# Mask rows on every eighth partition, and three larger mask transfers issued by ScalarE in place of nine by SyncE

## The chip, the cores and the metric

The kernel runs on one core of a Trainium2 chip. The metric is the device time of one execution in microseconds (us). A core has TensorE (PE: matrix products into PSUM), VectorE (DVE), ScalarE (ACT), GpSimd (POOL) and SyncE (SP, which here only issues DMAs), all running their own instruction streams in order and meeting at semaphores, and 16 DMA engines that all queues share.

## The reference, cut to what matters

```python
def _dcnv4(x, dw_w, dw_b, om_w, om_b, vp_w, vp_b, op_w):     # x: 8 images of 16 x 16 x 64
    xdw = depthwise_3x3(x, dw_w) + dw_b
    om = (xdw @ om_w + om_b).reshape(n, h, w, G, KK * 3)      # G = 8 groups, KK = 9 taps
    offset = om[..., :2 * KK].reshape(n, h, w, G, KK, 2)
    mask = om[..., 2 * KK:]
    value = (x @ vp_w + vp_b).reshape(n, h, w, G, GC)
    ...                                                       # bilinear sample of value at the offsets
    out = einsum('nhwgkc,nhwgk->nhwgc', sampled, mask).reshape(n, h, w, c)
    return out @ op_w

x = x + _dcnv4(groupnorm(x), ...)
t = x as tokens
t = t + attention(layernorm(t))
t = t + mixture_of_experts(layernorm(t))
```

The change touches only the convolution with offsets (`_dcnv4`), and of it the way in which `mask`, one number for each pixel, group and tap, comes from the product `om` to the place where it is multiplied in.

## The kernel before, in words

`conv_stage` works through the eight images one after the other; `token_stage` (attention and experts) follows behind a barrier. While image i is sampled, the tables of image i+1 are made, so each engine runs the same pattern once per image:

- PE (`image`, L445): nine steps v. Each has `sample(v)` (L382, or L387 for the last tap), which multiplies the x-interpolation weights `b` with the values `vt` into the PSUM ring `ps_t`; `reduce(v-1)` (L402, L406), which sums DVE's products; and two slots of `JOBS` for image i+1: the two halves of the offset product `om` (`offsets`, L292), the values (L303, on every second image), the output product of image i-1 (L314), and nine replications (`replicate`, L323) that spread offset rows over the partitions.
- DVE (`weight`, L684 and L688): 18 products w per image of `ps_t` with the y-interpolation weights in `a_rep`; two per step v. On every second image nine taps of the depthwise convolution (L658, L661) lie between them.
- ACT: `copy_offsets` (L508) brings `om` from PSUM to `om_f` with the bias; `high_offsets` (L516) rounds it to `om_r`; `copy_d` (L548); then for each replication a copy with absolute value (L530, L533) and a `hat` (L542), which turns it into a weight in `a` (y) or `b` (x).
- POOL: `low_offsets` (L756), the remainder of the rounding; `tables` (L767); and `masked(k)` (L777), which multiplies the taps of pair k of `a` by `mask`. Five pairs k hold the nine taps.
- SP: `masks(n)` (L247), nine DMAs that spread eight rows (one for each group) of `om_f` to all 128 partitions of `mask`, 128 KB each in elements of 1 KB; then `fill(n)` (L259), 20 DMAs that spread the masked `a` to `a_rep`, 16 of 256 KB in elements of 2 KB and four of 128 KB.

So the chain of one image is: `om` product, `om_f`, mask DMA and (beside it) replication and hat, `masked`, fill DMA, `weight`. `a`, `mask` and `om_f` have one buffer each; `a_rep` and `b` have two. `copy_offsets(0, n)` waits until the masks of image n-1 have been read (`mask_in`) and applied (`a_done`). The order on each engine is written out by hand. `P` is 128 partitions, `PIX` 256 pixels, `QUADS` 3.

Of the kernel before, what the change touches and what calls it, by code (L numbers as in the profile page):

```python
# [31 lines left out]
P = 128  # L32
IMAGES, H, W, C = 8, 16, 16, 64
PIX = H * W
TT = IMAGES * PIX // P
TPI = PIX // P
GROUPS = 8
GC = C // GROUPS
TAPS = 9
# [4 lines left out]
QUADS = 3  # L44
SLABS = IMAGES // 2
SELS = 6
ROWS = 120
BANK = 512
PAIRS = (TAPS + 1) // 2
BATCHES = TAPS  # L50
# [39 lines left out]
def conv_stage(nc, d, t_tok, pack, pack_in):  # L90

    with ExitStack() as ctx:
# [81 lines left out]
        a_hat = sem("a_hat")  # L175
        a_done = sem("a_done")
        b_done = sem("b_done")
        mask_in = [sem(f"mask_in{k}") for k in range(PAIRS)]
        a_filled = [[sem(f"a_filled{k}_{h}") for h in range(2)] for k in range(PAIRS)]
        sampled = sem("sampled")  # L180
        weighted = sem("weighted")
# [28 lines left out]

            return len(REPS) * n + r - len(BY_DVE)

        def mask_rows(k):

            return [(tap, tap // 3, (48, 56, 112)[tap % 3]) for tap in range(2 * k, min(2 * k + 2, TAPS))]

        def masks_in(k, images):

            return 16 * len(mask_rows(k)) * images

        def pair_taps(k):

            return slice(2 * k, min(2 * k + 2, TAPS))
# [7 lines left out]
        @block.sync  # L231
        def _(sp):
            sp.dma_start(x_turned[:, :, :, :].rearrange("p s y x -> p (s y x)"), d["x_turned"]).then_inc(x_in, 16)
            sp.dma_start(keep[:, :], d["keep"]).then_inc(keep_in, 16)
            sp.dma_start(start[:, :], d["start"]).then_inc(start_in, 16)
            sp.dma_start(t_tok[:, :, :], xview).then_inc(tokens_in, 16)
            sp.dma_start(pack[:, :], d["attention"]).then_inc(pack_in, 16)

            def masks(n):

                halves = [count(sp, 2 * n + half + 1) for half in range(2)]
                for k in range(PAIRS):
                    if k in (0, 3):
                        sp.wait_ge(om_copied, halves[k // 3])
                    for tap, q, row in mask_rows(k):
                        src = om_f[row:row + GROUPS, q, :]
                        sp.dma_start(mask[:, tap, :], src.unsqueeze(1).broadcast_to([GROUPS, P // GROUPS, PIX]))\  # L247
                          .then_inc(mask_in[k], 16)

            def fill(n, par):  # L250

                used = count(sp, WPI * (n - 1))
                if positive(used):
                    sp.wait_ge(weighted, used)
                for k in range(PAIRS):
                    sp.wait_ge(a_done, PAIRS * n + k + 1)
                    for m in range(DUOS):
                        src = a[32 * m:32 * m + 32, pair_taps(k), :]
                        sp.dma_start(a_rep[par][:, m, pair_taps(k), :],  # L259
                                     src.unsqueeze(1).broadcast_to([32, 4, src.shape[1], PIX]))\  # L260
                          .then_inc(a_filled[k][m // 2], 16)

            masks(0)
            fill(0, 0)
            masks(1)
            fill(1, 1)
            with sp.Fori(1, IMAGES // 2) as it:
                for par in range(2):
                    masks(2 * it + par)
                    fill(2 * it + par, par)  # L270

        @block.tensor
# [207 lines left out]
        def _(act):  # L480
# [16 lines left out]
            def copy_offsets(half, n):  # L497
                act.wait_ge(om_ps, 2 * n + half + 1)
                if positive(2 * n + half - 1):
                    act.wait_ge(om_low, 2 * n + half - 1)  # L500
                if positive(n):
                    for k in (range(3) if half == 0 else range(3, PAIRS)):
                        act.wait_ge(mask_in[k], masks_in(k, n))
                    if half == 0:
                        act.wait_ge(a_done, PAIRS * n)
                bank = ps_m[:, :] if positive(n) else ps_t[0][:, half, :]
                for q in range(2 - half):
                    op = act.activation(om_f[0:ROWS, 2 * half + q, :], bank[0:ROWS, q * PIX:(q + 1) * PIX],  # L508
                                        ACT.Identity, bias=om_bias[0:ROWS, 2 * half + q:2 * half + q + 1])
                op.then_inc(om_copied, 1)  # L510

            def high_offsets(half, n):
                act.wait_ge(om_copied, 2 * n + half + 1)
# [71 lines left out]
            def image(i, par, slab, made):  # L585
                n, npar = i + 1, 1 - par
                if made:
                    copy_offsets(0, n)
                    high_offsets(0, n)
                last = None if isinstance(i, int) and i == 0 else i - 1  # L590
                if LAG == 1 and last is not None:
                    copy_d(last)
                if made:
                    copy_offsets(1, n)
                    high_offsets(1, n)
                if LAG == 2 and last is not None:
                    copy_d(last)
                if made:
                    reps(n, npar, slab)
# [9 lines left out]
            high_offsets(0, 0)  # L609
            copy_offsets(1, 0)  # L610
            high_offsets(1, 0)
            first_reps()
            image(0, 0, 1, True)
            image(1, 1, None, True)
# [127 lines left out]
        @block.gpsimd  # L742
        def _(pool):
            pool.memset(minus_half[:, :], -0.5).then_inc(zeroed, 1)
            pool.memset(xpad[:, :, :, :], 0.0).then_inc(zeroed, 1)
            pool.wait_ge(zeroed, 2)
            pool.wait_ge(gn_steps, 5)
            pool.tensor_tensor(grstd[:, :], gvar_eps[:, :], minus_half[:, :], ALU.pow).then_inc(gn_pow, 1)

            def low_offsets(half, n):  # L750

                if half == 0 and positive(n):
                    pool.wait_ge(a_done, PAIRS * n)
                pool.wait_ge(om_high, 2 * n + half + 1)
                q = slice(2 * half, 2 + half)
                pool.tensor_tensor(om_r[64:ROWS, q, :], om_f[64:ROWS, q, :], om_r[64:ROWS, q, :].bitcast(F32),  # L756
                                   ALU.subtract).then_inc(om_low, 1)

            def tables(n, par, slab):

                pool.wait_ge(keep_in, 16)
                pool.wait_ge(om_low, 2 * n + 2)
                pool.wait_ge(v_done, slab + 1)
                if positive(WPI * (n - 1)):
                    pool.wait_ge(sampled, WPI * (n - 1))
                for j in range(DUO):
                    op = pool.tensor_tensor(vt[par][:, :, j, :, :].rearrange("p h y c -> p y h c"),  # L767
                                            v_sb[:, :, par, j, :].rearrange("p y (h c) -> p y h c", h=2),
                                            spread(spread(spread(rows[:, j], 1, H), 2, 2), 3, 4), ALU.mult)
                op.then_inc(vt_ready, 1)  # L770

            def masked(k, n, par):

                pool.wait_ge(a_hat, PAIRS * n + k + 1)
                pool.wait_ge(mask_in[k], masks_in(k, n + 1))
                v = a[:, pair_taps(k), :]
                pool.tensor_tensor(v, v, mask[:, pair_taps(k), :], ALU.mult).then_inc(a_done, 1)  # L777

            def image(n, par, slab):
                low_offsets(0, n)  # L780
                low_offsets(1, n)
                tables(n, par, slab)
                for k in range(PAIRS):
                    masked(k, n, par)

            image(0, 0, 0)
            image(1, 1, 0)
            image(2, 0, 1)
            with pool.Fori(1, IMAGES // 2 - 1) as it:
                image(2 * it + 1, 1, it)  # L790
                image(2 * it + 2, 0, it + 1)
            image(IMAGES - 1, 1, SLABS - 1)
# [736 lines left out]
def shape_arrays(np):  # L1529
# [10 lines left out]
    at = np.arange(P)  # L1540
    for which in range(SELS):
        for part in (0, 64):
            sel[part + 8 * which + at // 16, which, at] = 1.0
        if which < 3:
            sel[ROWS, which], sel[ROWS + 1, which] = -(at % 16), 1.0
        else:
# [4 lines left out]
    grid[ROWS + 2] = np.arange(W)[None, :]  # L1551
    kernel_at = np.zeros((P, QUADS), np.float32)
    for q in range(QUADS):
        for row, tap, kind in places(q):
            kernel_at[row:row + 8, q] = (tap % 3 - 1, tap // 3 - 1, 0)[kind]

    select = np.zeros((P, EXPERTS // 2, 2, C), np.float32)
    for e in range(EXPERTS):
# [8 lines left out]
def places(q):  # L1567

    y, x, m = 1, 0, 2
    spots = [(part + 8 * (3 * at + r), 3 * q + r, kind) for part in (0, 64) for at, kind in enumerate((y, x))  # L1570
             for r in range(3)]
    return spots + [(row, 3 * q + r, m) for r, row in enumerate((48, 56, 112))]

def laid_out(inputs, np):
# [6 lines left out]
    om_w = np.zeros((C, QUADS, P), om.dtype)  # L1582
    om_b = np.zeros((P, QUADS), bias.dtype)
    for q in range(QUADS):
        for row, tap, kind in places(q):
            j = 2 * TAPS + tap if kind == 2 else 2 * tap + kind
            om_w[:, q, row:row + 8] = om[:, :, j]
            om_b[row:row + 8, q] = bias[:, j]
    op = f["L0_conv_op_w"].reshape(DUOS, DUO, 2, 4, C).transpose(0, 2, 1, 3, 4)
    op_w = np.zeros((DUOS, 32, C), op.dtype)  # L1590
    op_w[:, 0:16] = op.reshape(DUOS, 16, C)
# [50 lines left out]
```

## Time and profile before

| | us |
|---|---|
| median of three runs | 498.77 (496.94 to 500.3) |
| the profiled execution, its own time | 497.56 |
| its span in the trace | 495.8 |
| PE, DVE, ACT, POOL busy | 409.9, 331.0, 238.3, 136.7 |

Of the span, the eight images of the convolution take what lies between the first DVE product at 35.3 us and the last at 292 us. The profiled execution is 1.2 us under the median; sums below are made against 497.56 and then moved to the median. A PE that is busy for 83% of the span is not a PE at its peak: its matmuls are pipelined, and the profile also shows stretches in which it was granted half its clock.

### The profile page before, as it was taken

To read this page: it belongs to the slowest core of one execution; us is meant where nothing else is said; L and a number is where in the kernel's file an instruction comes from. 1 tells how busy PE (TensorE), PEld (TensorE's weight loads), DVE (VectorE), ACT (ScalarE), POOL (GpSimd) and SP (SyncE) were. 2 spreads that over 40 slices of the span, in tenths; PEclk is the share of its full clock that TensorE was granted. 3 is DMA by queue.
4 is the path that set the end of the run, shared out by engine and by line. 5 is a ranking of instruction groups with operands and counts; after the bars stand their busy time and mean duration, and the time that the engine had idled before them with its cause. 6 is when DMAs were issued, how large, how long until landed. Compare 5 with 4: busy or idle time off the path is not lost. (4 is left out here: it accounts for less than half of the span.)

```text
span 495.8 us, 9559 instructions
## 1 busy us (share of the span) xinstructions
PE 409.9 (83%) x3188; PEld 223.2 (45%) x3188; DVE 331.0 (67%) x725; ACT 238.3 (48%) x528; POOL 136.7 (28%) x172
## 2 busy tenths in 40 slices
PE   0749969879799699895993854798999999999995
PEld 0612333322343233432330223586767767777673
DVE  3408937669488378693873864576876868667653
ACT  3542523435425235354260004457677676767752
POOL 1251240421502404215022004513323323233322
PEclk9958979989889789898896995569999999999998
DMA  6169488586684875966857705000000000000000
GB/s 207 39 156 236 122 210 204 125 226 166 164 238 111 208 201 117 231 157 163 220 123 201 210 14 240 1 1 1 1 1 13 2 0 3 12 0 3 12 0 13
DMA packets 38200, 53.94 MB, mean 109 GB/s; under 512 B 7440, under 2 KB 20880, under 8 KB 37904
## 3 DMA queue, kind: packets, MB, share of 16 engines
q1 hardware_dynamic: 38160, 53.44, 41.9%
q8 instruction: 22, 0.36, 0.3%
q14 instruction: 18, 0.15, 0.1%
HBM read 5.71 MB, written 0.52 MB: 13 GB/s over the span
## 5 line engine op out<-in xcount | busy, mean ns | idle before, releaser
L684 DVE TENSOR_TENSOR prod<-ps_t,a_rep 128x1024 f32<-128x1024 f32 x128 | 152.3, 1219 | 74.7 <-DMA a_rep<-a 55.1
L382 PE MATMUL ps_t<-b,vt 32*128 32x512 f32 x512 | 81.7, 710 | 13.8 <-DVE prod L684 13.6
L777 POOL TENSOR_TENSOR a<-a,mask 128x512 f32<-128x512 f32 (+1 forms) x40 | 46.7, 1170 | 155.2 <-DMA mask<-om_f 137.1
L402 PE MATMUL ps_d<-prod,keep 128*32 128x512 f32 x512 | 74.3, 655 | 2.7 <-DVE prod L684 2.5
L1231 POOL TENSOR_TENSOR total<-total,share 128x256 f32<-128x256 f32 x56 | 40.9, 731 | 87.3 <-DVE share L1125 86.9
L1109 DVE TENSOR_TENSOR hidden<-ps_h,gated 128x256 f32<-128x256 f32 x128 | 51.4, 415 | 3.7 <-ACT gated L1324 2.4
L1324 ACT ACTIVATE gated<-ps_h 128x256 f32<-128x256 f32 x128 | 47.9, 388 | 7.4 <-PE ps_h L1444 1.1
L530 ACT ACTIVATE a<-ps_m 128x512 f32<-128x512 f32 x28 | 16.7, 597 | 67.8 <-PE ps_m L323 67.8
L1444 PE MATMUL ps_h<-xf,w_h 128*128 128x256 f32 x128 | 43.7, 342 | 2.0 <-ACT gated L1324 2.0
L1125 DVE TENSOR_TENSOR share<-ps_yf,factor 128x256 f32<-128x256 f32 x56 | 23.7, 424 | 30.8 <-issue 12.8
L1318 ACT ACTIVATE factor<-ps_yf 128x256 f32<-128x256 f32 x64 | 24.7, 386 | 37.5 <-PE ps_yf L1479 37.5
L1479 PE MATMUL ps_yf<-hidden,w 128*64 128x256 f32 x256 | 41.9, 405 | 0.0
L323 PEld LDWEIGHTS ps_m<-om_r,sel 128*128 128x128 f32 x128 | 19.5, 192 | 48.3 <-issue 32.2
L382 PEld LDWEIGHTS ps_t<-b,vt 32*128 32x128 f32 x512 | 21.9, 198 | 42.0 <-DVE prod L684 29.8
L292 PE MATMUL ps_m<-conv,start 64*128 64x256 f32 x42 | 15.4, 479 | 26.5 <-ACT om_f L508 23.9
L1444 PE MATMUL ps_h<-xf,w_l 128*128 128x256 f32 x128 | 36.7, 287 | 0.0
L1444 PEld LDWEIGHTS ps_h<-xf,w_h 128*128 128x128 f32 x128 | 24.7, 193 | 26.6 <-issue 21.2
L1453 PE MATMUL ps_h<-xf,w_h 128*128 128x256 f32 x128 | 36.5, 286 | 0.0
L1453 PE MATMUL ps_h<-xf,w_l 128*128 128x256 f32 x128 | 36.4, 285 | 0.0
L323 PE MATMUL ps_m<-om_r,sel 128*128 128x256 f32 x128 | 32.6, 337 | 0.0
L530 ACT ACTIVATE b<-ps_m 128x512 f32<-128x512 f32 x28 | 16.7, 598 | 28.9 <-PE ps_m L323 28.9
L1475 PE MATMUL ps_yf<-dispatch,select 128*128 128x256 f32 x64 | 23.8, 371 | 5.8 <-DVE t_tok L1131 3.3
(149 smaller groups left out, 644.0 us busy)
## 6 DMA issues: line engine op xcount, KB each, us to landing
a_rep<-a SPq DMA_DIRECT2D x128, 256.0 KB, 4.6
mask<-om_f SPq DMA_DIRECT2D x72, 128.0 KB
a_rep<-a SPq DMA_DIRECT2D x32, 128.0 KB, 3.2
w_f<-in_w SPq DMA_DIRECT2D x2, 1024.0 KB, 5.7
start<-in_start SPq DMA_DIRECT2D x1, 960.0 KB, 7.3
x_turned<-in_x_turned SPq DMA_DIRECT2D x1, 512.0 KB, 3.4
t_tok<-in_x SPq DMA_DIRECT2D x1, 512.0 KB, 8.7
w<-in_w SPq DMA_DIRECT2D x1, 512.0 KB, 7.6
```

What stands on the lines that cost most here:

```text
L323: mm = pe.matmul(bank[:, s * PIX:(s + 1) * PIX], sel[:, tap % 3 + 3 * axis, :], om_r[:, tap // 3, :], start=True, stop=True)
L382: mm = pe.matmul(out, vt[par][r, v % 2, :, :, :].rearrange("p j y c -> p (j y c)"), b[par][r, pair_taps(v // 2), :].rearrange("p t x -> p ...
L402: mm = pe.matmul(ps_d[r, :], fold[:, v % 2, :], p, start=v == 0, stop=False, skip_group_check=True)
L530: act.activation(dst[:, pair_taps(k), :].rearrange("p t x -> p (t x)"), ps_m[:, :], ACT.Abs)\
L684: dve.tensor_tensor(p[:, :, :], t[:, :, :], a_rep[par][:, ms, pair_taps(v // 2), :].rearrange("p m t x -> p m (t x)"), ALU.mult).then_inc( ...
L777: pool.tensor_tensor(v, v, mask[:, pair_taps(k), :], ALU.mult).then_inc(a_done, 1)
L1109: dve.tensor_tensor(hidden[u % 4][:, :], ps_h2[u % 2][:, 0:PIX], gated[u % 4][:, :], ALU.mult)\
L1231: pool.tensor_tensor(sums[:, :], sums[:, :], share[p % 2][:, :], ALU.add).then_inc(added, 1)
L1324: act.activation(gated[u % 4][:, :], ps_h1[u % 2][:, 0:PIX], ACT.Silu).then_inc(silu_done, 1)
L1444: mm = pe.matmul(ps_h1[u % 2][:, 0:PIX], w[:, e, :], tokens, start=first, stop=not first)
L1453: mm = pe.matmul(ps_h2[u % 2][:, 0:PIX], w[:, e, :], tokens, start=first, stop=not first)
L1479: mm = pe.matmul(ps_y[64 * k:64 * k + 64, :], w3[:, u % EXPERTS, :], hidden[u % 4][:, :], start=True, stop=True)
```

## The change

The mask rows of `om_f` move. Before, tap t had its eight group rows on eight neighbouring partitions (48, 56 or 112 on), in column block t // 3. Now the rows of one third of the taps (three taps, one column block each) lie on partitions 0, 8, ..., 56, on 1, 9, ..., 57 or on 64, 71, ..., 113, and the offset rows take the partitions in between (`PLACE_ROWS`). Thus three taps are contiguous on a partition, and one DMA carries 3 KB elements for three taps: three DMAs an image of 384 KB each. They are issued by ACT, behind the rounding of the second half of the offsets, and wait for both halves. SP keeps the fills alone. Matmuls, activations and products keep their number and shapes.

```diff
+MASK_ROWS = [slice(0, 64, 8), slice(1, 64, 8), slice(64, 114, 7)]
+PLACE_ROWS = {0: [r for r in range(64) if r % 8 > 1], 64: [r for r in range(64, 120) if r % 7 != 1 or r > 113]}
...
-        mask_in = [sem(f"mask_in{k}") for k in range(PAIRS)]
+        mask_in = [sem(f"mask_in{j}") for j in range(QUADS)]
...
-            def masks(n):
-
-                halves = [count(sp, 2 * n + half + 1) for half in range(2)]
-                for k in range(PAIRS):
-                    if k in (0, 3):
-                        sp.wait_ge(om_copied, halves[k // 3])
-                    for tap, q, row in mask_rows(k):
-                        src = om_f[row:row + GROUPS, q, :]
-                        sp.dma_start(mask[:, tap, :], src.unsqueeze(1).broadcast_to([GROUPS, P // GROUPS, PIX]))\
-                          .then_inc(mask_in[k], 16)
...
             with sp.Fori(1, IMAGES // 2) as it:
                 for par in range(2):
-                    masks(2 * it + par)
                     fill(2 * it + par, par)
...
-                if positive(n):
-                    for k in (range(3) if half == 0 else range(3, PAIRS)):
-                        act.wait_ge(mask_in[k], masks_in(k, n))
-                    if half == 0:
-                        act.wait_ge(a_done, PAIRS * n)
+                if positive(n) and half == 0:
+                    for j in range(QUADS):
+                        act.wait_ge(mask_in[j], 16 * n)
+                    act.wait_ge(a_done, PAIRS * n)
...
+            def masks(n):
+
+                act.wait_ge(om_copied, 2 * n + 2)
+                for j in range(QUADS):
+                    src = om_f[MASK_ROWS[j], :, :].rearrange("g q x -> g (q x)")
+                    act.dma_start(mask[:, QUADS * j:QUADS * (j + 1), :].rearrange("p q x -> p (q x)"),
+                                 src.unsqueeze(1).broadcast_to([GROUPS, P // GROUPS, QUADS * PIX])).then_inc(mask_in[j], 16)
...
                 if made:
                     copy_offsets(1, n)
                     high_offsets(1, n)
+                    masks(n)
...
-                pool.wait_ge(mask_in[k], masks_in(k, n + 1))
+                for j in range(2 * k // QUADS, min(2 * k + 1, TAPS - 1) // QUADS + 1):
+                    pool.wait_ge(mask_in[j], 16 * (n + 1))
```

On SP, in the loop over images (`mask<-om_f` is a mask DMA, `a_rep<-a` a fill), one image began like this before:

```order
L247 DMA mask<-om_f 128x1x256 [waits om_copied]
L247 DMA mask<-om_f 128x1x256 x5
L244 REGISTER_ALU
L247 DMA mask<-om_f 128x1x256 [waits om_copied]
L247 DMA mask<-om_f 128x1x256 x2
L254 ISA
L256 ISA [waits weighted]
L259 DMA a_rep<-a 128x1x512 [waits a_done]
L259 DMA a_rep<-a 128x1x512 x3
```

Of these nine rows four stay, at the same place of SP's loop in the changed kernel:

```order
L248 UNCONDITIONAL_BRANCH
L248 ISA
L239 ISA [waits weighted]
L242 DMA a_rep<-a 128x1x512 [waits a_done]
L242 DMA a_rep<-a 128x1x512 x3
```

The nine mask issues are gone from SP; the fills keep their number, order and waits.

On ACT, at the seam between two images (`om_f` and `om_r` are the offsets and their rounding, `d_sb` the sums of the image before, `a<-ps_m` the first replication), the loop had before:

```order
L548 ACTIVATE d_sb<-ps_d 128x512 [waits out_ps]
L498 REGISTER_ALU
L503 REGISTER_ALU [waits mask_in3,om_low,om_ps]
L508 ACTIVATE om_f<-ps_m,om_bias 120x256 [waits mask_in4]
L516 ACTIVATE om_r<-om_f 120x256 [waits rep_ps,om_copied]
L522 REGISTER_ALU
L530 ACTIVATE a<-ps_m 128x512 [waits a_filled0_1,a_filled0_0,rep_ps]
```

And in the changed kernel:

```order
L535 ACTIVATE d_sb<-ps_d 128x512 [waits out_ps]
L478 REGISTER_ALU
L487 ACTIVATE om_f<-ps_m,om_bias 120x256 [waits om_low,om_ps]
L503 ACTIVATE om_r<-om_f 120x256 [waits rep_ps,om_copied]
L496 DMA mask<-om_f 128x1x768 [waits om_copied]
L496 DMA mask<-om_f 128x1x768 x2
L509 REGISTER_ALU
L512 REGISTER_ALU [waits rep_ps]
L517 ACTIVATE a<-ps_m 128x512 [waits a_filled0_1,a_filled0_0]
```

Three DMA issues stand now between the rounding of the second half and the copy of the first replication, and the waits for the masks of the image before have moved ahead of the first half.

## Rows read from the trace of the kernel before

**Rows 1.** Waits, whole span: us in total, times, longest

```profile
POOL a L777 <- DMA mask<-om_f: 137.1, 37, 19.1
DVE prod L684 <- DMA a_rep<-a: 55.1, 15, 11.1
```

**Rows 2.** Timeline of DVE: start, us, instruction, [idle before <-releaser]

```profile
35.31 1.22 DVE L684 TENSOR_TENSOR prod<-ps_t,a_rep 128x1024 f32<-128x1024 f32 x1 [11.15 <-DMA a_rep<-a]
...
142.52 2.36 DVE L684 TENSOR_TENSOR prod<-ps_t,a_rep 128x1024 f32<-128x1024 f32 x2 [0.72 <-PE ps_t L382]
...
167.02 1.23 DVE L684 TENSOR_TENSOR prod<-ps_t,a_rep 128x1024 f32<-128x1024 f32 x1 [6.47 <-DMA a_rep<-a]
...
176.38 1.23 DVE L684 TENSOR_TENSOR prod<-ps_t,a_rep 128x1024 f32<-128x1024 f32 x1 [1.67 <-PE ps_t L382]
...
267.05 1.23 DVE L684 TENSOR_TENSOR prod<-ps_t,a_rep 128x1024 f32<-128x1024 f32 x1 [8.22 <-DMA a_rep<-a]
269.06 1.22 DVE L684 TENSOR_TENSOR prod<-ps_t,a_rep 128x1024 f32<-128x1024 f32 x1 [0.79 <-DMA a_rep<-a]
```

**Rows 3.** Timeline of SP's DMA issues, merged by line

```profile
161.06 21.09 SPq L259 DMA_DIRECT2D a_rep<-a  x20
182.28 11.53 SPq L247 DMA_DIRECT2D mask<-om_f  x9
194.01 21.83 SPq L259 DMA_DIRECT2D a_rep<-a  x20
```

**Rows 4.** Tile mask: its issues' length in ns, min/median/max

```profile
L247 SPq DMA_DIRECT2D mask<-om_f x72: 619/1250/1847, 18.0 to 259.9; - x72
```

**Rows 5.** Windows: busy by engine, then PEclk, DMA share, GB/s

```profile
161.10:182.10 21.00, 16.50 (x92) 6.41 (x92) 10.82 (x13) 5.71 (x11) 5.68 (x7) 0.76 0.85 219
182.30:193.80 11.50, 10.75 (x82) 3.70 (x80) 11.43 (x13) 6.25 (x13) 2.55 (x2) 1.00 0.47 103
```

**Rows 6.** Timeline of PE round two seams between images

```profile
141.25 1.14 PE L382 MATMUL ps_t<-b,vt 32*128 32x512 f32 x8
...
159.90 1.14 PE L382 MATMUL ps_t<-b,vt 32*128 32x512 f32 x8
160.97 1.13 PE L292 MATMUL ps_m<-conv,start 64*128 64x256 f32 x4
162.03 1.09 PE L406 MATMUL ps_d<-prod,keep 128*32 128x256 f32 x16
166.45 0.70 PE L292 MATMUL ps_m<-conv,start 64*128 64x256 f32 x2 [3.33 <-ACT om_f L508]
168.30 2.09 PE L382 MATMUL ps_t<-b,vt 32*128 32x512 f32 x8 [1.16 <-DVE prod L684]
...
195.38 1.14 PE L382 MATMUL ps_t<-b,vt 32*128 32x512 f32 x8
...
202.54 1.94 PE L303 MATMUL ps_m<-keep,xv 128*32 128x32 f32 x128
...
205.48 1.10 PE L314 MATMUL ps_m<-keep,d_sb 128*128 128x64 f32 x8
```

**Rows 7.** Timeline of ACT: the prologue, then the seam at 165 us

```profile
20.93 0.60 ACT L557 ACTIVATE a<-ps_t 128x512 f32<-128x512 f32 x1 [1.49 <-PE ps_t L323]
...
34.61 0.84 ACT L508 ACTIVATE om_f<-ps_m,om_bias 120x256 f32<-120x256 f32 x2 [6.15 <-POOL a L777]
...
168.02 0.42 ACT L516 ACTIVATE om_r<-om_f 120x256 fp32r<-120x256 f32 x1
177.02 0.60 ACT L530 ACTIVATE a<-ps_m 128x512 f32<-128x512 f32 x1 [8.58 <-PE ps_m L323]
177.65 0.63 ACT L542 ACTIVATE a<-a 128x512 f32<-128x512 f32 x1
```

**Rows 8.** Timeline of POOL, first pair of the image of rows 7

```profile
188.33 1.28 POOL L777 TENSOR_TENSOR a<-a,mask 128x512 f32<-128x512 f32 x1 [18.03 <-DMA mask<-om_f]
```

**Rows 9.** Page, part 6: issues, KB each, median us to landing

```profile
a_rep<-a SPq DMA_DIRECT2D x128, 256.0 KB, 4.6
```

More of the change, by code:

```diff
@@ L211, in outs @@
             return len(REPS) * n + r - len(BY_DVE)
[L213 to L219, printed above, removed]
         def pair_taps(k):
@@ L261, in fill @@
                           .then_inc(a_filled[k][m // 2], 16)
-            masks(0)
             fill(0, 0)
-            masks(1)
             fill(1, 1)
@@ L611, in _ @@
             high_offsets(1, 0)
+            masks(0)
             first_reps()
@@ L1542, in shape_arrays @@
         for part in (0, 64):
-            sel[part + 8 * which + at // 16, which, at] = 1.0
+            sel[np.array(PLACE_ROWS[part])[8 * which + at // 16], which, at] = 1.0
         if which < 3:
@@ L1553, in shape_arrays @@
     for q in range(QUADS):
-        for row, tap, kind in places(q):
-            kernel_at[row:row + 8, q] = (tap % 3 - 1, tap // 3 - 1, 0)[kind]
+        for spots, tap, kind in places(q):
+            kernel_at[spots, q] = (tap % 3 - 1, tap // 3 - 1, 0)[kind]
     select = np.zeros((P, EXPERTS // 2, 2, C), np.float32)
@@ L1569, in places @@
     y, x, m = 1, 0, 2
-    spots = [(part + 8 * (3 * at + r), 3 * q + r, kind) for part in (0, 64) for at, kind in enumerate((y, x))
-             for r in range(3)]
-    return spots + [(row, 3 * q + r, m) for r, row in enumerate((48, 56, 112))]
+    spots = [(PLACE_ROWS[part][8 * (3 * at + r):8 * (3 * at + r + 1)], 3 * q + r, kind) for part in (0, 64)
+             for at, kind in enumerate((y, x)) for r in range(3)]
+    return spots + [(MASK_ROWS[j], 3 * j + q, m) for j in range(QUADS)]
 def laid_out(inputs, np):
@@ L1584, in laid_out @@
     for q in range(QUADS):
-        for row, tap, kind in places(q):
+        for spots, tap, kind in places(q):
             j = 2 * TAPS + tap if kind == 2 else 2 * tap + kind
-            om_w[:, q, row:row + 8] = om[:, :, j]
-            om_b[row:row + 8, q] = bias[:, j]
+            om_w[:, q, spots] = om[:, :, j]
+            om_b[spots, q] = bias[:, j]
     op = f["L0_conv_op_w"].reshape(DUOS, DUO, 2, 4, C).transpose(0, 2, 1, 3, 4)
```

## The prediction, on record before the changed kernel ran

> **What bounds the kernel now.** I read the waits first. The longest of the whole span is POOL's, for the mask DMA, and DVE's longest is for the fill [rows 1]: both ends of one DMA queue. So I followed that queue. SP's timeline has no hole [rows 3]: 20 fill issues from 161.06 us for 21.09 us, nine mask issues from 182.28 for 11.53, the next fill at 194.01. One turn is 32.95 us. DVE's first product of an image starts at 35.31 us for the first image and at 267.05 for the last [rows 2]: 231.74 / 7 = 33.11 us for an image. The queue's turn is the image's period; everything else waits for it.
>
> It is not the issuing itself that takes the time. A mask issue takes 0.62 us at least and 1.25 in the median [rows 4], so SP is held back while earlier transfers drain. And in the mask stretch the 16 DMA engines are busy for 0.47 of the time and move 103 GB/s, against 0.85 and 219 GB/s in the fill stretch [rows 5]. Transfers in one queue go in order, so for a third of the period half of the DMA capacity lies idle while the fills stand behind the masks.
>
> What the stall does further on: POOL stood ready for 18.03 us until the first mask came [rows 8], while the hat that it multiplies was done at 177.65 + 0.63 = 178.3 us [rows 7]. DVE then waited 6.47 us for the fill, and PE restarted slowly: a step of eight matmuls took 2.09 us at 168.30, 1.14 before and later [rows 2, 6, 7]. In that fill stretch the granted clock averages 0.76 against 1.00 in the mask stretch [rows 5], that is, part of it ran at 1.2 GHz and not 2.4, after PE had stood still.
>
> **The period when DMA is not late.** I put it together from full-clock pieces of PE [rows 6], sample(0) of an image to sample(0) of the next. From sample(0) to sample(2): 1.07 us (159.90 to 160.97), the first offset product 1.06, the last reduce 1.09, then the second offset product, which must wait for ACT's 0.84 us copy [rows 7]: I put its end 0.2 us after the reduce. Then 0.70, sample(1) 1.07, reduce(0) another 1.09, the output product 1.10 less the 0.07 by which steps overlap (159.90 + 1.14 against 160.97): 7.3 us in all. On odd images the values add 1.94. From sample(2) to the next sample(0) nothing waits for DMA today: 141.25 to 159.90 is 18.65 us on an odd image. On an even one, with DVE's nine convolution taps, the product w4 starts at 176.38 [rows 2]; w4 follows sample(2) by 1.27 us (142.52 against 141.25), so it is 175.11 to 195.38, 20.27 us. Odd: 7.3 + 1.94 + 18.65 = 27.9. Even: 7.3 + 20.27 = 27.6. Mean 27.75 us, against 33.11: **5.36 us an image, seven times: 37.5 us.**
>
> **Is the DMA then fast enough?** The sum of engine time in rows 5: the fill is 0.85 x 21.0 = 17.9 us on all 16. If the 0.47 of the mask stretch means about half of the engines fully busy, the masks are 0.94 x 11.5 = 10.8 us on that half. If the two overlap, the busier half has 28.7 us of work an image, even if 3 KB elements gain nothing. That is 1 us over 27.75, and there is a lead to eat first: pair 0 was ready for masking at 178.3 and its fill went out at 194.01 [rows 3, 7]. With masks there early the fill goes out by about 180, some 14 us sooner, while DVE's turn comes only 5.4 us sooner. Some 8 us of lead against 1 us an image lasts through eight images. I take nothing for it; the bound above is 7 us.
>
> **What moves to ACT.** Three issues after the rounding of the second half, ahead of the first replication's copy. No row shows a DMA issued by ACT. The nearest rows are SP's: three at 0.62 are 1.9 us, at 1.25 3.75 us, at 1.85 5.5 us [rows 4]. What hides them: ACT sat idle for 8.58 us at just this place [rows 7], but most of that was PE standing still. Without the stall it is shorter. The rounding ends 1.3 us after the second offset product (168.44 against 167.15 [rows 6, 7]). The first replication's copy starts 0.64 us after w4 (177.02 against 176.38 [rows 2, 7]), so 1.9 us after sample(2) starts. Between lie sample(1), reduce(0) and the output product: ACT has 1.07 + 1.09 + 1.03 + 1.9 - 1.3 = 3.8 us on even images and 5.7 on odd ones. At the median nothing is lost, at the longest 1.7 us on each of four even images; queued behind a late ACT stand the first replication's copy, through it PE's next use of `ps_m`, and the hat for POOL. I take 1 us for all images, with bounds of 0 and 7.
>
> **Ends of the stage.** First image: ACT's rounding ends at 20.93 - 1.49 = 19.44 us, where SP began the masks at 18.0 [rows 4, 7], and ACT has those 1.49 us idle for 1.9 us or more of issues. The fills no longer stand behind nine masks, which draws DVE's first product forward. But the offsets of image 1 wait for POOL's last masking (34.61 us [rows 7]), and that for about the same mask bytes. I take 0, with bounds of 3 us either way. Last image: the 0.79 us wait for a fill at 269.06 goes [rows 2]: 0.8 us. The waits for three `mask_in` that moved ahead of the first half are met long before, and matmuls, activations and products are the same: nothing. The token stage is untouched.
>
> **Sum.** 37.5 + 0.8 - 1 = 37.3 us. From the profiled execution's 497.56 that is 460.3; the median is 1.2 above it, so **461 us**.
>
> **Rivals.** A: the DMA engines stay the bound. The fill's share of 0.85 speaks for it [rows 5]: there is little room beside the fills, and if the masks take that room one for one the turn stays fill plus mask. The mask part would be at most today's 11.5 us and at least its bytes at the fill's rate, 1.18 MB / 219 GB/s = 5.4 us (then there is no bound). The middle, 9.5 us, gives 21.4 + 9.5 = 31 us an image, 15 us gained, **484 us**; with 11.5 us the change does nothing, 498. Against it: the idle half in the mask stretch.
>
> The Trainium skill has the rule for this rival (DMA: Bandwidth & Descriptors, section Issuing engines are not separate DMA queues): transfers from several engines run on the same 16 DMA engines and interleave, so a second issuer saves only sequencer time. By that rule the result is A. The trace does not bear out its premise in the mask stretch, where the share is 0.47. My estimate from that page is 3.6 + 3.6 + 2.1 = 9.3 us for the three DMAs alone, where nine took 11.5; no row here shows the new layout.
>
> B: ACT becomes the late one, and the time ends **slower**. Place: the third issue at each seam. Mechanism: ACT's queue takes an issue only when the one before has landed. A 256 KB fill lands 4.6 us after its issue [rows 9]; at no less for 384 KB ACT is held 0.6 + 2 x 4.6 = 9.8 us, 6.0 more than the even images have and 4.1 more than the odd ones: 5.05 us an image, nearly the whole gain. Each such stall also leaves PE at half clock for a while, as today; I put that at 2 us a seam, two steps at 2.09 for 1.14, so 498.8 - 37.3 + 7 x 7.05 = **511 us**. It turns slower where ACT is held for more than 4.75 + 5.36 - 2 = 8 us on average. Against it: SP today takes three issues in less than that with 1.25 us in the median.
>
> C: the masks go out as said, but ACT is held at its upper bound and the 28.7 us bind as well: 461 + 6 (beyond the 1 us taken) + 7 = **474 us**.
>
> **How the numbers follow.** Forecast (450 to 470): 0.60. A: 0.22, a quarter of it within 1% of 498.8. B: 0.08, a quarter of it within 1%. C: 0.07. Faster than 450, if the steps at the seam overlap better than my chain of PE: 0.03. 1%, or 5 us, is about what a measurement of this kernel can tell from no change. So faster 0.60 + 0.16 + 0.07 + 0.03 = 0.86, same 0.08, slower 0.06. For the range, the lower bound is 461 less 3 us at the first image, 1 us of ACT and 1 us a seam: 450. Up it takes in C and the better half of A, to 486: above lie 0.11 of A and 0.08 of B.
>
> **What would show it.** SP's timeline should have fills only, with pauses between images in which it waits for POOL. POOL's wait for the mask DMA should fall from 137 us to under 30, and DVE's waits for `a_rep` to the first image alone. PE's full-clock stretches should join, and DVE's first products should be 27 to 29 us apart. The first copy of a replication on ACT should follow the mask issues with little or no PE wait behind it. SP without a pause and a period of 30 us or more would mean A; a PE wait for ACT's copy at `ps_m` at each seam would mean B or C. I am wrong if the periods at the seams contain a wait that DMA now hides, such as POOL's remainder of the rounding ahead of the first replication.

## The result, and the profile after

The changed kernel took 480.0 us in the median of four runs (479.04 to 481.95), the kernel before 499.53 us on the same chip: a ratio of 0.9615, with a 95% interval of 0.9556 to 0.9674. The time lies inside the whole range of 450 to 486 us, but outside the forecast's own 450 to 470, and the gain is 19.5 us where 37.8 were forecast, about half. Of the cases, rival A (the DMA engines stay the bound, 484 us) is the nearest. The profiled execution took 481.95 us, the longest of the four; its span is 480.0, 15.8 under the span before, and it is these 15.8 us that are accounted for below.

The waits of the changed kernel (us in total, times, longest) answer to [rows 1]:

```profile
POOL a L767 <- DMA mask<-om_f: 74.6, 17, 6.5
DVE prod L673 <- PE ps_t L362: 43.0, 44, 9.3
ACT a L517 <- DMA a_rep<-a: 37.8, 7, 7.2
ACT a L517 <- issue: 33.5, 6, 6.6
...
PEld ps_m L303 <- ACT a L517: 27.7, 12, 5.8
```

POOL's wait for the masks fell from 137.1 us to 74.6, not to under 30, and DVE's 55.1 us of waiting for `a_rep` are no longer among the long ones. Two new waits stand before ACT's first copy of a replication. One is for its own DMA issues (`issue`). The other is for fills: `a` has one buffer, and the copy into it must wait until the fill of the image before has read it. PE then waits for ACT at `ps_m`, and DVE for PE at `ps_t`.

SP's timeline, from the first fill to the last, and from the first fill of the last image, answers to [rows 3]:

```profile
26.40 236.95 SPq L242 DMA_DIRECT2D a_rep<-a  x160
...
242.18 21.17 SPq L242 DMA_DIRECT2D a_rep<-a  x20
```

And SP's waits for the masked `a` (total, times, longest):

```profile
SPq L242 <- POOL a L767: 24.1, 8, 17.6
```

The longest of these waits, 17.6 us, stands before the first fill; the other seven are 6.5 us together, so from then on SP issues 160 fills almost without a pause. From the first fill of the first image to that of the last is (242.18 - 26.40) / 7 = **30.8 us an image**; only the last image, with no masks beside it, still takes 21.17 us, as the fills did alone [rows 3]. The masks are gone from SP's queue, and the turn of the fills has become longer by 30.8 - 21.2 = 9.6 us an image, against 11.53 us when the masks stood in front of them. The tile `mask` (length of its issues in ns, min/median/max), now on ACT, answers to [rows 4]:

```profile
L496 ACTq DMA_DIRECT2D mask<-om_f x24: 602/1329/4411, 19.2 to 225.7; - x24
```

ACT's timeline at a seam answers to [rows 7]:

```profile
131.99 6.72 ACTq L496 DMA_DIRECT2D mask<-om_f  x3
...
138.96 0.60 ACT L517 ACTIVATE a<-ps_m 128x512 f32<-128x512 f32 x1 [6.56 <-issue]
...
150.76 0.60 ACT L517 ACTIVATE a<-ps_m 128x512 f32<-128x512 f32 x1 [5.05 <-DMA a_rep<-a]
```

The queue does hold ACT: one issue takes up to 4.41 us, three take 6.72. Now DVE's first products of the first and of the last image, which answer to [rows 2]:

```profile
33.69 1.23 DVE L673 TENSOR_TENSOR prod<-ps_t,a_rep 128x1024 f32<-128x1024 f32 x1 [9.34 <-PE ps_t L362]
...
69.03 2.36 DVE L673 TENSOR_TENSOR prod<-ps_t,a_rep 128x1024 f32<-128x1024 f32 x2
...
252.87 4.81 DVE L673 TENSOR_TENSOR prod<-ps_t,a_rep 128x1024 f32<-128x1024 f32 x4 [0.56 <-PE ps_t L362]
```

The period is (252.87 - 33.69) / 7 = 31.3 us, before 33.11 and forecast 27.75. The first of the seven took 35.3 us (to 69.03, the first product of the second image), the other six 30.6 in the mean, the turn of the fills. That is 12.6 us gained in seven periods. The first product comes 1.6 us earlier (35.31 to 33.69), and from the last image's first product to the end of the span it is 480.0 - 252.87 = 227.1 us against 495.8 - 267.05 = 228.75, another 1.6. Together 15.8 us, the difference of the two spans. Last, three windows answer to [rows 5]: one over more than five images, one in which masks are in flight beside the fills (their packets run from 134.6 to 148.7 us), and one in which the fills are alone:

```profile
75.00:250.00 175.00, 154.69 (x1358) 59.45 (x1352) 133.46 (x131) 75.52 (x147) 49.87 (x52) 0.96 0.82 192
...
135.20:149.20 14.00, 13.20 (x95) 4.18 (x94) 11.33 (x11) 4.62 (x8) 3.98 (x4) 1.00 0.79 177
119.00:132.00 13.00, 10.76 (x86) 4.65 (x86) 10.46 (x11) 8.82 (x19) 3.00 (x3) 1.00 0.87 211
```

And the DMA queues of the page (packets, MB, time as a share of 16 engines' span):

```profile
q1 hardware_dynamic: 28368, 44.00, 37.6%
q10 hardware_dynamic: 3264, 9.44, 8.1%
```

Beside the masks the two kinds of transfer together move 177 GB/s at a share of 0.79, less than the fills do alone (211 GB/s, 0.87), and the masks' packets are in flight for 14.6 us of each image (images 1 to 7, by the times of the 3 KB packets). Queue q10, ACT's, holds the masks only: 0.081 x 16 x 480.0 / 8 = 77.8 us of engine time an image.

### The profile page after: what moved, and what is told of

The parts are those of the page before. It is cut to its first block and busy times, and to the rows that moved or that the text cites. A ratio compares the mean times of both kernels' runs of the same rounds, so it can differ in the third digit from the quotient of the medians.

```text
span 480.0 us, 9496 instructions
## 1 busy us (share of the span) xinstructions
PE 401.7 (84%) x3188; PEld 221.1 (46%) x3188; DVE 332.5 (69%) x725; ACT 237.4 (49%) x528; POOL 136.7 (28%) x172
## 5 line engine op out<-in xcount | busy, mean ns | idle before, releaser
L362 PE MATMUL ps_t<-b,vt 32*128 32x512 f32 x512 | 77.8, 678 | 2.9 <-DVE prod L673 2.7
L382 PE MATMUL ps_d<-prod,keep 128*32 128x512 f32 x512 | 71.9, 634 | 6.6 <-DVE prod L673 6.4
L767 POOL TENSOR_TENSOR a<-a,mask 128x512 f32<-128x512 f32 (+1 forms) x40 | 46.9, 1179 | 104.3 <-DMA mask<-om_f 74.6
L517 ACT ACTIVATE a<-ps_m 128x512 f32<-128x512 f32 x28 | 16.7, 597 | 85.3 <-DMA a_rep<-a 37.8
L303 PEld LDWEIGHTS ps_m<-om_r,sel 128*128 128x128 f32 x128 | 20.3, 200 | 68.3 <-ACT a L517 27.7
L303 PE MATMUL ps_m<-om_r,sel 128*128 128x256 f32 x128 | 33.8, 347 | 17.5 <-ACT a L517 17.5
L1308 ACT ACTIVATE factor<-ps_yf 128x256 f32<-128x256 f32 x64 | 24.6, 385 | 37.9 <-PE ps_yf L1469 37.9
L362 PEld LDWEIGHTS ps_t<-b,vt 32*128 32x128 f32 x512 | 21.2, 192 | 29.7 <-DVE prod L673 17.7
L745 POOL TENSOR_TENSOR om_r<-om_f,om_r 56x512 fp32r<-56x512 f32 (+1 forms) x16 | 15.9, 1002 | 57.3 <-ACT om_r L503 57.2
```

What stands on the lines that cost most here:

```text
L303: mm = pe.matmul(bank[:, s * PIX:(s + 1) * PIX], sel[:, tap % 3 + 3 * axis, :], om_r[:, tap // 3, :], start=True, stop=True)
L362: mm = pe.matmul(out, vt[par][r, v % 2, :, :, :].rearrange("p j y c -> p (j y c)"), b[par][r, pair_taps(v // 2), :].rearrange("p t x -> p ...
L382: mm = pe.matmul(ps_d[r, :], fold[:, v % 2, :], p, start=v == 0, stop=False, skip_group_check=True)
```

## The experiments

Theory A: the DMA engines bound the period, and the masks take room from the fills one for one; then the masks' cost is set by what they cost the engines, above all by where their source rows lie. Theory B: ACT, held by its issues, starts the replications late. Theory C: the one buffer of `a` makes ACT wait for the fills, and a second one gives the time back. Theory P, which the later expectations test, is a form of A: the DMA engines that carry a mask meet at the ports through which they read its rows. Each of the ten runs was timed in three rounds beside the kernel before on the same chip.

**The floor: masks for the first image alone.** The masks of images 1 to 7 are not sent; those of image 0 stay in `mask`.

```diff
-                    masks(n)
...
-                    pool.wait_ge(mask_in[j], 16 * (n + 1))
+                    pool.wait_ge(mask_in[j], 16)
```

> Leaves out the mask DMAs of images 1 to 7 (they are multiplied with the masks of image 0). Theory A, the DMA engines are the bound (fills alone take some 21 us an image in the kernel before, 29.6 with masks beside them in the changed one): the fills fit again, SP pauses between images, and DVE's first products come 27 to 28.5 us apart instead of 31.3, some 455 us. Theory B, ACT's hold of 6.7 us on its three issues is the bound: the same 455, for the hold goes too; only SP's pauses and the waits for a_rep differ. Theory C, the single buffer a is the bound whatever the masks do (copy of the first factor waits for the fill of the image before): little change, 475 to 480, ACT still waits for a_rep. If it stays over 460 my chain of PE steps at the seam (27.75 us an image) was wrong too.

456.16 us, ratio 0.9132 (0.9094 to 0.917). SP's timeline, the fills of the last image:

```profile
211.60 20.89 SPq L242 DMA_DIRECT2D a_rep<-a  x20
```

DVE's timeline, the first products of the first and of the last image:

```profile
33.72 1.23 DVE L672 TENSOR_TENSOR prod<-ps_t,a_rep 128x1024 f32<-128x1024 f32 x1 [9.33 <-PE ps_t L362]
...
227.07 4.81 DVE L672 TENSOR_TENSOR prod<-ps_t,a_rep 128x1024 f32<-128x1024 f32 x4 [0.61 <-PE ps_t L362]
```

SP's waits for the masked `a`:

```profile
SPq L242 <- POOL a L766: 57.1, 11, 19.2
```

And a window (busy by engine, PEclk, DMA share, GB/s):

```profile
75.00:220.00 145.00, 138.64 (x1275) 53.07 (x1271) 124.67 (x122) 71.96 (x139) 46.29 (x48) 1.00 0.71 174
```

The period is (227.07 - 33.72) / 7 = 27.6 us: the chain of PE that the prediction put together (27.75) is the bound once DMA is out of the way, at a granted clock of 1.00. The last image's fill starts 15.5 us ahead of its first product, against 10.7 us in the changed kernel (252.87 - 242.18) and 7.3 in its first image (33.69 - 26.40). So here the fills run ahead, and SP pauses: 37.9 us in ten waits behind the first, against 6.5 in the changed kernel. Theory C, which expected 475 to 480 us, is already against this; A and B are not parted, for ACT's issues went together with the transfers.

**Two buffers of `a`.** The changed kernel with `a` doubled by the image's parity, and semaphores of the fills for each.

```diff
-        a = sb("a", [P, TAPS, PIX])
+        a = [sb(f"a{i}", [P, TAPS, PIX]) for i in range(2)]
...
```

> Two buffers for a, used by turns, so that a copy of a replication waits for the fill two images back. Theory A: the queue of fills still needs 29.6 us an image with masks beside it, SP has no pause, but the lag can now build up over several images: 29.6 to 30 us an image at most, 466 to 470 us, ACT's waits for a_rep gone and DVE's waits for a_rep back in their place. Theory B: ACT's hold stays, 476 to 480. Theory C: the full forecast, 455 to 462.

480.2 us, ratio 0.9626 (0.9583 to 0.9668): no change against 480.0. ACT's waits for `a_rep` are gone from the list, and SP's issues take as long as before:

```profile
26.35 236.36 SPq L242 DMA_DIRECT2D a_rep<-a  x160
```

Theory C falls: the wait for the buffer was only the form in which the late fills showed. Theory A's own number for this run, 466 to 470 us, was missed; the time stands in theory B's range of 476 to 480, and it takes the issues spread, below, to part the two.

**The mask rows back on neighbouring partitions.** Still three DMAs of 3 KB elements, issued by ACT.

```diff
+MASK_ROWS = [slice(48, 56), slice(56, 64), slice(112, 120)]
+PLACE_ROWS = {0: list(range(48)), 64: list(range(64, 112))}
```

> Undoes the spreading alone: the mask rows back on eight neighbouring partitions (48, 56 and 112 on), still three DMAs of 3 KB elements issued by ACT. If the place of the rows matters to the transfer, the masks take longer in flight than 14.4 us and hold the fills more: with the 11.3 us of the kernel before in place of the 8.9 that they now cost the fills, 2.4 us an image, 495 us. If it does not matter: 480 within 3.

549.15 us, ratio 1.0976 (1.0917 to 1.1034): 69 us slower than the changed kernel, with the same bytes, DMAs and issuer, and far beyond both expected numbers (480 and 495). SP's timeline, all fills and those of the last image:

```profile
29.91 302.47 SPq L242 DMA_DIRECT2D a_rep<-a  x160
...
310.57 21.81 SPq L242 DMA_DIRECT2D a_rep<-a  x20
```

The masks' queue on the page:

```profile
q10 hardware_dynamic: 3264, 9.44, 12.8%
```

The turn of the fills is (310.57 - 29.91) / 7 = 40.1 us, and 0.128 x 16 x 547.8 / 8 = 140 us of engine time an image for the masks, against 77.8.

**The new rows and sizes, issued by SP as before.** `masks(n)` stands ahead of `fill(n)` in SP's loop again.

```diff
+                    sp.dma_start(mask[:, QUADS * j:QUADS * (j + 1), :].rearrange("p q x -> p (q x)"),
...
+                    masks(2 * it + par)
                     fill(2 * it + par, par)
...
-                    act.dma_start(mask[:, QUADS * j:QUADS * (j + 1), :].rearrange("p q x -> p (q x)"),
...
```

> Undoes the move to ACT alone: three DMAs of 3 KB elements from spread rows, issued by SP at the old place, all before the fills of the image. If the size and the place of the rows shorten the masks by themselves, the mask stretch of SP falls from 11.3 to some 9 us and the period from 33.1 to 31: about 484. If only the second queue helps: 498 within 4.

477.59 us, ratio 0.9549 (0.95 to 0.9599), no slower than the changed kernel, and better than the 484 that was expected. SP's timeline:

```profile
141.10 4.08 SPq L238 DMA_DIRECT2D mask<-om_f  x3
148.05 22.73 SPq L250 DMA_DIRECT2D a_rep<-a  x20
170.92 3.93 SPq L238 DMA_DIRECT2D mask<-om_f  x3
```

The window of the mask stretch between two fills:

```profile
141.10:148.00 6.90, 6.90 (x52) 1.76 (x48) 5.92 (x6) 4.10 (x9) 1.26 (x1) 1.00 0.53 120
```

The turn shown is 170.92 - 141.10 = 29.8 us, and the mean of seven turns 30.4, although masks and fills stand in one queue. So the part of the change that moved the issues from SP to ACT brought nothing; the whole gain is in the three DMAs and their rows.

**ACT's issues spread.** The second and third issue stand behind the first and the second replication.

```diff
+                    if r in (1, 2):
+                        masks(n, [r])
...
-                    masks(n)
+                    masks(n, [0])
```

> The three issues on ACT no longer stand together: the first behind the rounding, the second behind the first replication's copy, the third behind the third replication's. Theory B, ACT's hold of 6.7 us at the seam costs PE time: the hold shrinks to 2 or 3 us in pieces and the time falls to about 470. Theory A, the DMA engines are the bound and the hold is covered by them: 480 within 3, SP without a pause as before.

481.06 us, ratio 0.9664 (0.9589 to 0.974). The tile's issues:

```profile
L496 ACTq DMA_DIRECT2D mask<-om_f x24: 601/612/2471, 19.5 to 229.3; - x24
```

The median issue is 0.61 us in place of 1.33, the longest 2.47 in place of 4.41, and the time is the same. Theory B falls: holding ACT cost nothing while the DMA was late anyway. (The spread also sends two of the masks later; the next run, with the three issues together again, says the same without that.)

**Rows on every fourth partition, issued by ACT.**

```diff
+MASK_ROWS = [slice(0, 32, 4), slice(1, 32, 4), slice(64, 96, 4)]
+PLACE_ROWS = {0: [r for r in range(64) if r >= 32 or r % 4 > 1], 64: [r for r in range(64, 120) if r >= 96 or r % 4]}
```

> As the changed kernel, with the mask rows on every fourth partition (0 to 28, 1 to 29, 64 to 92). Theory P, the masks cost the fills time because several of the eight engines that carry a mask read over the same SBUF ports: with a port for each row the masks' stay in flight falls from 14.4 us to under 11, the fills take 27 to 28 us an image with masks beside them, 460 to 468 us. Rival, they cost it because eight engines carry mask and fill in turn, whatever the ports: 480 within 3.

455.96 us, ratio 0.9138 (0.9065 to 0.9211): 24 us faster than the changed kernel, on the floor of 456.16 and below the 460 to 468 that theory P expected. SP's timeline, all fills and those of the last image:

```profile
25.90 215.23 SPq L242 DMA_DIRECT2D a_rep<-a  x160
...
218.15 22.99 SPq L242 DMA_DIRECT2D a_rep<-a  x20
```

The same window as for the floor:

```profile
75.00:220.00 145.00, 137.99 (x1267) 53.04 (x1263) 122.60 (x122) 71.02 (x138) 45.99 (x47) 1.00 0.87 214
```

The masks' queue on the page:

```profile
q10 hardware_dynamic: 3264, 9.44, 6.7%
```

The turn of the fills is (218.15 - 25.90) / 7 = 27.5 us, just under PE's 27.75, and the rate beside the masks is 214 GB/s where the changed kernel moved 192. The masks cost 0.067 x 16 x 455.8 / 8 = 61 us of engine time an image.

**The same rows, issued by SP.** The rows of this and the issuer of the fourth experiment.

> The same rows with the three DMAs issued by SP at the old place. Theory P: the stretch from the first mask issue to the first fill falls from 7.2 us to some 5 and the turn of SP from 30.3 to 28, 462 to 467 us, where 477.6 was measured with rows on every eighth partition. Rival, masks that run alone are not limited by the ports but by landing and by POOL: 477 within 3.

454.32 us, ratio 0.9132 (0.9061 to 0.9203), below the expected 462 to 467: the same as with ACT, although here the masks stand ahead of the fills. SP's timeline:

```profile
129.72 2.58 SPq L238 DMA_DIRECT2D mask<-om_f  x3
136.12 20.47 SPq L250 DMA_DIRECT2D a_rep<-a  x20
156.73 2.65 SPq L238 DMA_DIRECT2D mask<-om_f  x3
```

The window of the mask stretch:

```profile
129.70:136.00 6.30, 6.30 (x50) 2.14 (x46) 5.54 (x6) 3.33 (x6) 1.20 (x1) 1.00 0.54 151
```

The turn shown is 27.0 us, the mean of seven 27.5; the mask stretch moves 151 GB/s at nearly the share of 0.53 that moved 120.

**Nine DMAs from the rows of the changed kernel, issued by SP.** Against the kernel before the rows differ, and with them the order in which they are read (three DMAs in a row from one set); all nine also wait for both halves of the offsets.

```diff
+                for tap in range(TAPS):
+                    src = om_f[MASK_ROWS[tap // 3], tap % 3, :]
+                    sp.dma_start(mask[:, tap, :], src.unsqueeze(1).broadcast_to([GROUPS, P // GROUPS, PIX]))\
+                      .then_inc(mask_in[tap // 3], 16)
...
```

> Nine DMAs of 1 KB elements as in the kernel before, from the spread rows (every eighth partition), issued by SP. It parts the place of the rows from the size of the elements. If the place alone brings the gain: 478 to 482. If the size alone: 495 to 499. If each brings part: between, some 488.

481.29 us, ratio 0.9656 (0.9583 to 0.9729): nearly the whole gain of the change, with DMAs no larger than before. So the gain comes with the rows, not with the size.

**Three DMAs from neighbouring partitions, issued by SP.** The 24 rows are those of the kernel before, and so is the issuer; what differs is the size of the DMAs, with it which taps lie on one row and are read together, and that all wait for both halves.

> The mask rows on eight neighbouring partitions as in the kernel before, SP issues as before, only three DMAs of 3 KB elements in place of nine of 1 KB. If the size of the elements brings nothing by itself: 495 to 501. If larger elements shorten the masks: 485 to 492. If one DMA from few partitions at a time is slower than several from different ones in flight together: over 505.

561.21 us, ratio 1.1254 (1.1165 to 1.1344): with these rows the larger DMAs are a loss of 63 us against the 498.47 measured beside them. Against the new rows in the same three DMAs from SP (477.59), where the rows alone differ, they are a loss of 84 us. SP's timeline:

```profile
141.50 6.56 SPq L238 DMA_DIRECT2D mask<-om_f  x3
152.24 28.88 SPq L250 DMA_DIRECT2D a_rep<-a  x20
181.66 6.50 SPq L238 DMA_DIRECT2D mask<-om_f  x3
```

The window of the mask stretch, which moves 78 GB/s at a share of 0.51:

```profile
141.50:152.20 10.70, 10.30 (x73) 3.11 (x73) 10.63 (x12) 5.67 (x12) 1.26 (x1) 1.00 0.51 78
```

**Rows on every sixteenth partition, issued by SP.** If distance were what helps, this would be better than every eighth.

```diff
+MASK_ROWS = [slice(0, 128, 16), slice(1, 128, 16), slice(2, 64, 8)]
```

> As the kernel with rows on every fourth partition issued by SP, but two of the three row sets on every sixteenth partition over all 128 (0 to 112, 1 to 113) and one on every eighth (2 to 58). Theory P, ports: these rows meet on four ports as those on every eighth partition do: 475 to 481, as measured with every eighth. Rival, distance between the rows is what counts: 454 or less, for the rows lie four times as far apart as in the kernel at 454.

502.5 us, ratio 1.0075 (1.0037 to 1.0113): worse than every eighth by 25 us. It is not distance, which expected 454 or less. But theory P's number, 475 to 481, was missed as well. SP's timeline, where a fill behind the masks takes 25.11 us:

```profile
154.16 4.04 SPq L238 DMA_DIRECT2D mask<-om_f  x3
161.50 25.11 SPq L250 DMA_DIRECT2D a_rep<-a  x20
186.74 4.11 SPq L238 DMA_DIRECT2D mask<-om_f  x3
```

The trace also holds each DMA packet with its length. For the four kernels in which SP issues three mask DMAs an image, of the 3072 packets of 3 KB in the run the commonest length and how many have it; then, of images 1 to 7, the median of each of the three DMAs (896 packets each, taken in order of time) and the mean of all; how long an image's mask packets are in flight, from the start of the first to the end of the last, in us; the period by DVE's first products; and the kernel's time in us:

```
rows on                  commonest      1st   2nd   3rd DMA   mean     flight   period   time
neighbouring             453 ns, 1107   453   453   233 ns    370 ns   22.1     40.6     561.21
every sixteenth          233,    1586   233   233   233       247      15.2     33.5     502.5
every eighth (seventh)   233,    1279   233   233   181       217      11.2     30.3     477.59
every fourth             121,     629   134   164   192       174       8.4     27.5     454.32
```

The period follows the flight: from row to row the flight falls by 6.9, 4.0 and 2.8 us, the period by 7.1, 3.2 and 2.8. So the place of the rows seems to act through the time for which the masks are in flight.

The commonest lengths stand on steps, 121, 233 and 453 ns: 112 ns for the first step and 2 x 110 for the second. So it looks as if a packet has to itself, or shares with one other or with three, something that passes 3072 bytes in 110 to 112 ns, some 27 to 28 GB/s. The third DMA on every seventh partition has a lower median than its two neighbours on every eighth. The trace agrees in the sizes of the steps and in the rate, and the order of the four kernels is that of the counts. It does not agree throughout: the third DMA from neighbouring rows has a median of 233 ns with two ports counted, like the other two, and with every fourth row the medians lie above 121.
## Why the prediction was right and wrong

**The bound now: right.** The queue that held masks ahead of fills set the period, and taking the masks away gave PE's chain: 27.75 us forecast, 27.6 with no masks beyond the first image's, (228.48 - 32.50) / 7 = 28.0 with every fourth row on ACT, by DVE's first products there:

```profile
32.50 2.47 DVE L673 TENSOR_TENSOR prod<-ps_t,a_rep 128x1024 f32<-128x1024 f32 x2 [8.50 <-DMA a_rep<-a]
...
228.48 3.68 DVE L673 TENSOR_TENSOR prod<-ps_t,a_rep 128x1024 f32<-128x1024 f32 x3 [0.56 <-PE ps_t L362]
```

That the mean came out so well is in part luck: without masks the single periods run from 25.4 to 29.4 us, by DVE's first products of all images, where the sum had 27.6 and 27.9.

**"Is the DMA then fast enough?": the step that failed.** It put 28.7 us of work on the busier half of the engines and took nothing for it. The turn of the fills was 30.8 us in its place, 3.05 over PE's chain. Three things in the step were wrong.

First, the fill was entered with its busy time, 0.85 x 21.0 = 17.9 us, as if the idle 15% were room for masks. It was not: with masks beside them fills and masks together moved 177 GB/s, where the fills alone moved 211. The masks' part was about right (10.8 us forecast; 77.8 / 8 = 9.7 us if they sit on half of the engines, as the shares near 0.5 of all mask stretches suggest). With the fill at its whole turn the sum is 21.2 + 9.7 = 30.9 us, and the measured turn is 30.8. That is rival A's premise, one for one, and its 31 us. The sum was made after the result, and that it meets to 0.1 us is partly luck: made in the same way for the other rows with ACT's issues it gives 21.2 + 61 / 8 = 28.8 against a turn of 27.5 (every fourth), and 21.2 + 140 / 8 = 38.7 against 40.1 (neighbouring). Rival A's own 9.5 us was luck too: it was called the middle of 5.4 and 11.5, but that is 8.5, which by the same sum would have given 476 us and not 484.

Second, the lead of 8 us did not exist. It came from a pair that would be ready for its fill 14 us sooner, but such a pair then stands behind the fill of the image before on SP, whose queue was full from the first image on. From the first fill to the first product it was 7.3 us at the start and 10.7 at the end; without masks it grew from 7.3 to 15.5, so the 8 us of the forecast came only where the fills had room.

Third, the even split into halves hid what the cost of the masks depends on. The idle half of the engines in the mask stretch was read as room that a second queue could use. The runs show that the mask DMAs were slow because of the rows that they read, and that this could be mended where they stood, in SP's queue.

In numbers: 37.5 us were forecast from seven periods and 12.6 came. Of the 24.9 missing, (30.8 - 27.75) x 7 = 21.4 are the fill's turn, and 10.7 - 7.3 = 3.4 the distance of the products behind it, which grew in the first period (35.3 us). What made that first period long is not shown. The ends gave 1.6 us at the first image, inside its bounds of 3, and 1.6 at the last, where 0.8 was counted.

**ACT: near enough in its sum, with a longer hold than its rows.** Three issues took 6.7 us at the seam shown, more than the 5.5 of the upper bound; the rows it came from were issues of 128 KB. That cost nothing here, by the spread issues, and no more than the runs can tell once DMA is not late: 455.96 us with ACT, 454.32 with SP, and their intervals overlap. Rivals B and C fall by that. Of the signs that the prediction named, those of two cases came: SP almost without a pause and a period over 30 us, for A, and PE's wait for ACT's copy at `ps_m` (27.7 us), for B or C. The second sign misled: neither sparing ACT the hold (the spread issues) nor sparing it the wait for the fills (two buffers) gave any time back.

**The page's rule.** The prediction set the rule of the Trainium skill (DMA: Bandwidth & Descriptors, section Issuing engines are not separate DMA queues) against the share of 0.47 and gave it 0.22. The rule was right: 480.0 us from ACT, 477.59 from SP. The share had been read wrongly: that half of the engines' time is idle behind the masks does not show that fills beside the masks would be as fast as alone.

**What stays open.** Why nine small DMAs from neighbouring rows (103 GB/s [rows 5]) do better than three large ones (78 GB/s) was not tried by itself. In the kernel before, successive DMAs take rows from 48, 56 and 112 on in turn, so different rows are in flight together; with three, all engines stay longer on one set. That would explain it, but is only argued. The fills behind the masks take 20.5 us with every fourth row, 22.7 with every eighth and 28.9 with neighbouring ones, and the masks' packets are still in flight for the first 4.2, 5.6 and 12.0 us of them, in the images shown. How a mask packet slows a fill packet, and why every sixteenth row does so much worse than every eighth, is open. No run tried to bring the masks onto more of the engines: the share stayed near 0.5 in every mask stretch, whatever the rows.

## What to carry to other kernels

An idle share of the DMA engines in one stretch is not by itself room for a second queue: here a second queue gained nothing with either set of rows (480.0 us against 477.59, 455.96 against 454.32). When forecasting an overlap of transfers, also work the sum with the whole turn of the one, not its busy time, added to the other, and do not count on a lead before it has built up. In a broadcast from a few partitions the place of the source rows can matter more than the size of the transfer or the engine that issues it: with SP issuing three DMAs, eight rows on every fourth partition gave 454 us, on every eighth 478, on every sixteenth 502, on neighbouring ones 561. Farther apart is not always better. Leave the suspected transfer out once, early: that run gives the floor (456 us), and shows how much of a forecast gain is there to be had.

## What the runs showed of the hardware

The commonest lengths of a packet that reads a broadcast row stand on steps: 121, 233 and 453 ns for 3 KB, by the rows' places. Making the DMAs three times larger, which also changes the order in which rows are read, made the kernel slower where the rows are neighbours (498.47 to 561.21 us). Masks and fills in flight together moved less than the fills alone (177 GB/s against 211). And a compute engine that issues DMAs is held by them: the third 384 KB issue of an image kept ACT for up to 4.41 us, where the first of the three takes 0.61 to 0.64 from the second image on.
